# A hybrid attention kernel: order of the head, four constant products, and three instead of four products for each group of experts

## The chip, the cores and the metric

The kernel runs on one core of a Trainium2 chip. The metric is device microseconds (us) of one execution. A core has five engines that work side by side and wait for each other through semaphores: TensorE (PE, the matrix products), VectorE (DVE), ScalarE (ACT), GpSimd (POOL) and SyncE (SP, which only issues DMAs here). PE's products go to PSUM; the other engines bring them from there to SBUF.

## What is computed

```python
x = x + wo @ (softmax(k.T q) v)          # q, k, v = wq x, wk x, wv x: 32 channels; 4 images, 64 channels, 1024 pixels
t = tokens(x)                            # 4 x 1024 tokens of 64
u = layernorm(t);  t = t + softmax(u u.T) u
w = layernorm(t);  p = softmax(w @ router_w + router_b)        # 8 experts
top_p, top_i = top_k(p, 2);  top_p = top_p / sum(top_p)
t = t + sum over the two of top_p * (w @ expert_w[top_i] + expert_b[top_i])
```

All is fp32 in and out. A product that must be near fp32 is made of several products of rounded parts: a number is split into a high part (rounded) and a low part (the rest).

## The kernel before

The four images b = 0 to 3 go through the same stages, staggered: while PE makes the first attention of one image it makes the maxima, the second attention or the experts of others. The order on every engine is written out by hand, one call after another. Each engine works off its calls in that order.

**The ring.** Most of PE's results go into a ring of three PSUM buffers of two banks each. `ORDER` lists every use of the ring in PE's order; use n has buffer n mod 3, and `take` lets PE wait until the reader of use n - 3 is done. So the order in `HEAD`, `FIRST` and so on must be that of PE's calls, and it fixes for each use whose release it waits for.

**The head (image 0, and the start of image 1).** `project_qk` makes q or k of an image: two halves of 512 columns, two products each. `project_v(b, a)` makes one half of v together with the transposed input: eight products of 96 columns into `acc1` or `acc2`. `max_scores` makes a tile of scores whose row maxima DVE takes (`row_max`). When all eight tiles of an image are done, DVE negates the maxima (`negate_max`, semaphore `s_nm`), PE turns them into a row (`max_row` on PE, eight products of 128 columns), and ACT and DVE copy one half of that row each (`max_row` on ACT and DVE, `s_mrow`). Then `scores1(b, j)` can start, ACT takes exponentials (`exp1`), and `weigh_pair1` multiplies two tiles of them by v.

A projected q or k is rounded by ACT (`round_q`, `round_k`, `s_qr`, `s_kr`), then DVE writes the low part (`split_q`, `split_k`, `s_qs`, `s_ks`); only then can `max_scores` of that image start. ACT's `values(b, a)` brings a half of v out of PSUM (two copies, `s_vx`). DVE's order in the head stays: `row_max` of image 0, `negate_max(0)`, `split_q(1)`, `max_row(0)`, `split_k(1)`, two small copies of wo (behind PE's `transpose` into `acc2`), then `row_max(1, ...)`.

`keep_clock(n)` issues n products of constants (512 columns, f16) into `acc1` that nobody reads. It is called at the very start; `acc1` and `acc2` are free behind `wait_ge(s_vx, 4 * B)`.

**The experts.** `experts(b, g)` makes 128 x 1024 numbers: for two token tiles (h = 0, 1) the products with all 8 experts. Its operands are `w_hi`, `w_lo` (tokens) and `e1`, `e2` (expert weights); the half h has 64 rows of its own and a bank of its own. There are 16 such groups, four in each image. DVE's `weigh_experts(b, g)` multiplies a group by the gates (`s_prod`); POOL adds the experts up (`sum_pair`, then `residual`, which gives `y`) for images 0 and 1, and `y_transposed(b)` brings y back on PE. For images 2 and 3 PE adds the experts up itself (`add_experts`), with POOL or DVE halving them first. The gates come from `route(b)` on PE and `top2(b)`, some twenty small instructions on DVE. `w_transposed(b)` waits for the second norm: `att2_transposed` on PE, `tokens2`, `stats_of_2` on DVE, a power on POOL (`rstd`), `normalize2` on DVE.

Of the kernel before, what the change touches and what calls it, by code (L numbers as in the profile page):

```python
# [24 lines left out]
P = 128  # L25
# [13 lines left out]
def per_tile(name, b):  # L39
    return [(f"{name}{t}", b) for t in range(T)]  # L40

HEAD = [("w3", 0), ("q", 0), ("k", 0)] + per_tile("mx", 0) + [("q", 1), ("k", 1), ("mr", 0)]

FIRST = [("st0", 0), ("st1", 0), ("mx0", 1), ("st2", 0), ("mx1", 1), ("st3", 0), ("mx2", 1), ("mx3", 1), ("st4", 0),
         ("mx4", 1), ("st5", 0), ("mx5", 1), ("st6", 0), ("mx6", 1), ("st7", 0), ("mx7", 1), ("mr", 1), ("po", 0)]
# [22 lines left out]
TAIL = [("e1", 2), ("e2", 2), ("wT", 3), ("e3", 2), ("rt", 3), ("e0", 3), ("e1", 3), ("e2", 3), ("e3", 3)]  # L70
ORDER = HEAD + FIRST + SECOND + THIRD + FOURTH + FIFTH + SIXTH + SEVENTH + EIGHTH + TAIL
PLACE = {use: (n % RING, n) for n, use in enumerate(ORDER)}
# [6 lines left out]
def col(tile):  # L79
    return (tile % 2) * CHUNK + (tile // 2) * P  # L80


def build(nc, x, wq, wk, wv, wo, rw, rb, ew, eb, out):
    ctx = ExitStack()
    with ctx:
        def sb(name, shape, dt=F32):
            return ctx.enter_context(nc.sbuf_tensor(name, shape, dt))
# [4 lines left out]
        def two(name, shape, dt=F32):  # L92
            return [sb(f"{name}_{n}", shape, dt) for n in range(2)]
# [9 lines left out]
        w3 = sb("w3", [ROW, 2, C])  # L103
# [7 lines left out]
        e1 = sb("e1", [P, E * C], F32R)  # L111
        e2 = sb("e2", [P, E * C], F32R)
# [22 lines left out]
        w_hi = two("w_hi", [P, CHUNK], F32R)  # L135
        w_lo = two("w_lo", [P, CHUNK], F32R)
# [137 lines left out]
        def filled(engine, name, b):  # L274
            buf, n = PLACE[(name, b)]
            engine.wait_ge(s_fill, n + 1)
            return ring[:, buf]

        def flat(buf):
            return buf.rearrange("p a n -> p (a n)")  # L280
# [147 lines left out]
        def _(pe):  # L428
            taken = iter(range(len(ORDER)))

            def take(name, b):
                buf, n = PLACE[(name, b)]
                assert n == next(taken), (name, b)
                if n >= RING:
                    pe.wait_ge(*release(*ORDER[n - RING]))
                return ring[:, buf]

            def project_qk(name, b):
                which = "qk".index(name)
                buf = take(name, b)  # L440
                if b:
                    pe.wait_ge(s_xs, b + 2)
                for h in range(2):
                    if b == 0 and which == 0:
                        pe.wait_ge(s_xs, h + 1)
                    rows = xst[b][:, h * CHUNK:(h + 1) * CHUNK]
                    pe.matmul(buf[0:ROW, h, :], w1[:, which].rearrange("p r m -> p (r m)"), rows, start=True, stop=False)  # L447
                    mm = pe.matmul(buf[0:ROW, h, :], w2[:, which].rearrange("p r m -> p (r m)"), rows, start=False, stop=True)
                    if b == 0 and h == 0:
                        mm.then_inc(s_qk0, 1)  # L450
                mm.then_inc(s_fill, 1)

            def project_v(b, a):

                bank = v_at[a]
                if b:
                    pe.wait_ge(s_xs, b + 2)
                    pe.wait_ge(s_vx, 4 * (b - 1) + 2 * a + 2)
                for t in range(T // 2):
                    tile = a * (T // 2) + t  # L460
                    toks = xst[b][:, col(tile):col(tile) + P]
                    o = t * (M + C)
                    pe.matmul(bank[:, o:o + M + C], toks, vx1[:, :], start=True, stop=False)
                    mm = pe.matmul(bank[:, o:o + M + C], toks, vx2[:, :], start=False, stop=True)
                mm.then_inc(s_vp, 1)

            def max_scores(b, tile):
                buf = take(f"mx{tile}", b)
                if tile == 0:
                    pe.wait_ge(s_qs, b + 2)  # L470
                    pe.wait_ge(s_ks, b + 2)
                home = b % 2
                for h in range(2):
                    mm = pe.matmul(buf[:, h, :], kst[home][0:ROW, col(tile):col(tile) + P],  # L474
                                   qst[home][0:ROW, h * CHUNK:(h + 1) * CHUNK], start=True, stop=True)
                mm.then_inc(s_fill, 1)

            def max_row(b):
                buf = take("mr", b)
                pe.wait_ge(s_nm, 2 * (b + 1))  # L480
                for tile in range(T):
                    c = col(tile)
                    mm = pe.matmul(flat(buf)[0:ROW + 2, c:c + P], nmax[:, tile, :], ident_r[:, :], start=True, stop=True)  # L483
                mm.then_inc(s_fill, 1)

            def scores1(b, j):
                buf = take(f"st{j}", b)
                if j == 0:
                    pe.wait_ge(s_mrow, 2 * (b + 1))
                home = b % 2  # L490
                for h in range(2):
                    mm = pe.matmul(buf[:, h, :], qst[home][0:ROW + 2, col(j):col(j) + P],  # L492
                                   kst[home][0:ROW + 2, h * CHUNK:(h + 1) * CHUNK], start=True, stop=True)
                mm.then_inc(s_fill, 1)
# [108 lines left out]
            def experts(b, g):  # L603

                buf = take(f"e{g}", b)
                products = [(w, e) for w in (w_hi[b % 2], w_lo[b % 2]) for e in (e1, e2)]
                for n, (w, e) in enumerate(products):
                    for h in range(2):
                        rows = slice(h * C, (h + 1) * C)
                        mm = pe.matmul(buf[:, h, :], w[rows, g * P:(g + 1) * P], e[rows, :], start=(n == 0), stop=(n == 3))  # L610
                mm.then_inc(s_fill, 1)

            def gates_transposed(b):
# [36 lines left out]
            buf = take("w3", 0)  # L650
# [18 lines left out]
            project_v(2, 1)  # L669
            max_scores(0, 7)  # L670
            project_qk("q", 1)
            project_qk("k", 1)
            project_v(3, 0)
            max_row(0)
            project_v(3, 1)


            scores1(0, 0)
            scores1(0, 1)
            pe.wait_ge(s_wol, 2 * 16)  # L680
            pe.wait_ge(s_vx, 4 * B)
            pe.transpose(acc2[:, 0:C], wo4[:, :, :].rearrange("p a m -> p (a m)"), ident[0:C, 0:C]).then_inc(s_woT, 1)
            max_scores(1, 0)
            scores1(0, 2)
            weigh_pair1(0, 0)
# [95 lines left out]
            scores2(1, 4)  # L781
            weigh_pair2(1, 2)
            experts(0, 0)
            scores2(1, 5)
            u_transposed(2)
            max_scores(3, 7)
            experts(0, 1)
            scores2(1, 6)
            weigh_pair2(1, 4)
            experts(0, 2)  # L790
            scores2(1, 7)
            max_row(3)
# [101 lines left out]
        def _(act):  # L894
# [4 lines left out]
            def round_q(b):  # L899
                act.activation(qst[b % 2][0:ROW, :], flat(filled(act, "q", b))[0:ROW, :], ACT.Copy).then_inc(s_qr, 1)  # L900

            def round_k(b):
                act.activation(kst[b % 2][0:ROW, :], flat(filled(act, "k", b))[0:ROW, :], ACT.Copy).then_inc(s_kr, 1)

            def values(b, a):
                act.wait_ge(s_vp, 2 * b + a + 1)
                tiles = slice(a * (T // 2), (a + 1) * (T // 2))
                b4 = v_at[a][:, 0:(T // 2) * (M + C)].rearrange("p (t c) -> p t c", c=M + C)
                act.activation(val[b][:, tiles, 0:M], b4[:, :, 0:M], ACT.Copy).then_inc(s_vx, 1)
                act.activation(xt[b][:, tiles, :], b4[:, :, M:M + C], ACT.Copy).then_inc(s_vx, 1)  # L910

            def max_row(b):
                buf = filled(act, "mr", b)
                act.activation(kst[b % 2][ROW:ROW + 2, 0:CHUNK], buf[ROW:ROW + 2, 0, :], ACT.Copy).then_inc(s_mrow, 1)
# [56 lines left out]
            buf = filled(act, "w3", 0)  # L971
# [4 lines left out]
            for name, dst, s_rounded in (("q", qst[0], s_qr), ("k", kst[0], s_kr)):  # L976
                k, used = PLACE[(name, 0)]
# [14 lines left out]
            values(2, 0)  # L992
            values(2, 1)
            round_q(1)
            round_k(1)
            values(3, 0)
            max_row(0)
            values(3, 1)

            for j in range(4):  # L1000
                exp1(0, j)
# [3 lines left out]
            for h in range(2):  # L1005
                rows = slice(h * C, (h + 1) * C)
# [104 lines left out]
            b = B - 1  # L1111
# [336 lines left out]
```

## Time and profile before

| | us |
|---|---|
| median of 3 runs (208.2, 208.34, 466.2) | 208.34 |
| the profiled execution: its own time | 209.9 |
| its span, first to last instruction | 207.8 |
| PE busy in it | 195.0 |
| DVE busy | 142.5 |
| ACT busy | 108.3 |
| POOL busy | 62.9 |

The profile is one execution recorded by the hardware. Its span leaves out what lies before the first and behind the last instruction. A matmul's end in it is modelled and products overlap, so a row's duration is longer than the step from one product to the next; "busy" counts overlapping instructions once. The mean granted TensorE clock over the span is 0.992 of full speed.

### The profile page before, as it was taken

How to read it: one execution, taken by the hardware profiler on the slowest of the kernel's cores; microseconds unless marked ns; L12 is line 12 of the kernel's file. 1: busy time of each engine (PE TensorE's matmuls, PEld its weight loads, DVE VectorE, ACT ScalarE, POOL GpSimd, SP SyncE). 2: the span in 40 equal slices, each digit the busy share in tenths (PEclk: the TensorE clock that was granted, in tenths of full speed). 3: DMA queues.
4: the chain of work that ended last, by engine and by line, in shares of the span. 5: the costliest groups of instructions: out<-in, count | busy, mean ns of one | idle time of the engine just before them, and what ended most of it. 6: DMA issues, size and time to landing. Idle time of an engine off the chain costs nothing.

```text
span 207.8 us, 3044 instructions
## 1 busy us (share of the span) xinstructions
PE 195.0 (94%) x1121; PEld 100.0 (48%) x1121; DVE 142.5 (69%) x359; ACT 108.3 (52%) x172; POOL 62.9 (30%) x79
## 2 busy tenths in 40 slices
PE   7899999999999899998989999899999999899993
PEld 2678634354434334433433554353444334377882
DVE  3889736778846994793688855628794361998980
ACT  3765825548945466564367456566563875301010
POOL 8394000003000300021003479700369760026160
PEclk9999979999999999999999999999999999999999
DMA  4890000000000000000000000110000002000021
GB/s 112 204 156 0 3 0 0 2 2 3 0 0 0 0 3 0 0 0 3 0 2 0 3 2 0 24 26 0 3 0 3 0 0 52 0 3 0 0 54 51
DMA packets 3502, 3.69 MB, mean 18 GB/s; under 512 B 2208, under 2 KB 2464, under 8 KB 3488
## 3 DMA queue, kind: packets, MB, share of 16 engines
q1 hardware_dynamic: 3248, 3.45, 7.5%
q8 instruction: 9, 0.15, 0.3%
q10 hardware_dynamic: 240, 0.05, 0.1%
q14 instruction: 5, 0.04, 0.1%
HBM read 2.45 MB, written 1.05 MB: 17 GB/s over the span
## 4 chain that ended last, share of the span: by engine, by line
PE 66%; DVE 22%; POOL 4%; issue 3%; ACT 2%; DMA 1%; SPq 0%; DVEq 0%; POOLq 0%
PE acc L499 20%; PE ring L563 9%; PE ring L610 6%; PE ring L474 6%; DVE rowmax L1136 6%; PE ring L492 5%; POOL sm L372 4%; PE acc L640 3%; PE ring L536 2%; DVE stats L1169 2%; PE ring L547 2%; PE ring L599 2%; PE ring L483 2%; DVE tok L1215 2%; PE ring L447 1%
## 5 line engine op out<-in xcount | busy, mean ns | idle before, releaser
L372 POOL TENSOR_TENSOR sm<-sm,minus_half 128x8 f32<-128x8 f32 x8 | 15.8, 1975 | 117.2 <-DVE sm L1179 117.2
L920 ACT ACTIVATE prob<-ring,shift 128x1024 f32<-128x1024 f32 x32 | 35.6, 1112 | 25.0 <-PE ring L563 24.7
L1136 DVE TENSOR_REDUCE rowmax<-ring 128x1 f32<-128x1024 f32 x32 | 38.0, 1218 | 13.9 <-PE ring L474 13.8
L917 ACT ACTIVATE prob<-ring 128x1024 f32<-128x1024 f32 x32 | 32.1, 1023 | 21.3 <-PE ring L492 21.0
L499 PE MATMUL acc<-prob,val 128*64 128x512 f32 x128 | 31.8, 619 | 0.0
L499 PE MATMUL acc<-prob,u 128*64 128x512 f32 x128 | 31.2, 606 | 0.2 <-ACT prob L920 0.2
L1275 DVE TENSOR_TENSOR prod<-ring,gate 128x1024 f32<-128x1024 f32 x16 | 19.3, 1219 | 6.7 <-PE ring L610 6.7
L474 PE MATMUL ring<-qst,kst 96*128 96x512 f32 x64 | 22.3, 436 | 1.0 <-DVE rowmax L1136 0.8
L492 PE MATMUL ring<-kst,qst 98*128 98x512 f32 x64 | 21.8, 431 | 0.9 <-DVE kst L1133 0.5
L563 PE MATMUL ring<-zsw,zst 64*128 64x512 f16 x64 | 19.4, 376 | 0.0
L563 PE MATMUL ring<-zst,zsw 64*128 64x512 f16 x64 | 19.2, 376 | 0.0
L492 PEld LDWEIGHTS ring<-kst,qst 98*128 98x128 f32 x64 | 10.7, 193 | 11.8 <-ACT prob L917 5.9
L499 PEld LDWEIGHTS acc<-prob,val 128*64 128x64 f32 x128 | 7.9, 139 | 16.1 <-issue 13.3
L499 PEld LDWEIGHTS acc<-prob,u 128*64 128x64 f32 x128 | 7.7, 136 | 15.6 <-issue 12.9
L474 PEld LDWEIGHTS ring<-qst,kst 96*128 96x128 f32 x64 | 10.2, 190 | 9.1 <-issue 4.0
L384 POOL TENSOR_TENSOR half<-prod 128x512 f32<-128x512 f32 x8 | 10.6, 1322 | 8.4 <-DVE prod L1275 8.2
L563 PE MATMUL ring<-zst 64*128 64x512 f16 x32 | 12.3, 386 | 0.7 <-DVE rowmax L1136 0.4
L610 PE MATMUL ring<-e,w_hi 64*128 64x512 f32 x64 | 12.4, 443 | 0.0
L563 PE MATMUL ring<-zsw 64*128 64x512 f16 x32 | 12.4, 386 | 0.0
L610 PE MATMUL ring<-e,w_lo 64*128 64x512 f32 x64 | 10.9, 394 | 0.0
L563 PEld LDWEIGHTS ring<-zst 64*128 64x128 f16 x32 | 3.0, 92 | 13.3 <-issue 6.5
L423 POOL TENSOR_TENSOR prod<-prod 128x512 f32<-128x512 f32 x6 | 7.6, 1278 | 5.8 <-DVE prod L1275 4.8
(160 smaller groups left out, 323.3 us busy)
## 6 DMA issues: line engine op xcount, KB each, us to landing
xin<-in_x SPq DMA_DIRECT2D x6, 256.0 KB, 4.9
out<-ob SPq DMA_DIRECT2D x6, 128.0 KB, 2.5
xin<-in_x SPq DMA_DIRECT2D x4, 128.0 KB, 2.8
e_in<-in_L_ffn_expert_w SPq DMA_DIRECT2D x2, 128.0 KB
out<-ob SPq DMA_DIRECT2D x4, 64.0 KB, 2.0
eb_in<-in_L_ffn_expert_b SPq DMA_DIRECT2D x8, 2.0 KB
wo<-in_L_conv_wo SPq DMA_DIRECT2D x2, 8.0 KB, 2.2
r_in<-in_L_ffn_router_w SPq DMA_DIRECT2D x2, 2.0 KB
```

The lines of the kernel that those rows point to most:

```text
L372: pool.tensor_tensor(sm[:, 3, :], sm[:, 2, :], minus_half[:, :], ALU.pow).then_inc(s_rs, 1)
L384: pool.tensor_tensor(half[:, :, :, :], p[:, 0:E // 2], p[:, E // 2:E], ALU.add).then_inc(s_half, 1)
L423: pool.tensor_tensor(prod[:, g, 0:E // 2], prod[:, g, 0:E // 2], prod[:, g, E // 2:E], ALU.add).then_inc(s_half, 1)
L474: mm = pe.matmul(buf[:, h, :], kst[home][0:ROW, col(tile):col(tile) + P], qst[home][0:ROW, h * CHUNK:(h + 1) * CHUNK], start=True, stop=True)
L492: mm = pe.matmul(buf[:, h, :], qst[home][0:ROW + 2, col(j):col(j) + P], kst[home][0:ROW + 2, h * CHUNK:(h + 1) * CHUNK], start=True, stop= ...
L499: mm = pe.matmul(acc[h * C:(h + 1) * C, :], stationary[:, j, :], prob[:, j % DEEP, h * CHUNK:(h + 1) * CHUNK], start=(j == 0), stop=(j == ...
L563: mm = pe.matmul(buf[:, h, :], held[h][rows, col(j):col(j) + P], moving[h][rows, h * CHUNK:(h + 1) * CHUNK], start=(n == 0), stop=(n == 2))
L610: mm = pe.matmul(buf[:, h, :], w[rows, g * P:(g + 1) * P], e[rows, :], start=(n == 0), stop=(n == 3))
L917: act.activation(prob1[:, j % DEEP, :], flat(filled(act, f"st{j}", b)), ACT.Exp).then_inc(s_p1, 1)
L920: act.activation(prob2[:, j % DEEP, :], flat(filled(act, f"s{j}", b)), ACT.Exp, bias=shift[:, :], accum_out=rsum2[b % 2][:, j:j + 1]).then ...
L1136: dve.tensor_reduce(rowmax[:, tile:tile + 1], flat(filled(dve, f"mx{tile}", b)), AX.X, ALU.max).then_inc(s_mx, 1)
L1275: dve.tensor_tensor(prod[:, g].rearrange("p e h c -> p h e c"), buf.rearrange("p h (e c) -> p h e c", c=C), gates, ALU.mult).then_inc(s_pr ...
```

## The change

Three edits. In the head, PE makes k of image 1 behind `max_row(0)`, and both halves of v of image 3 ahead of it; `HEAD` and ACT's list follow. Behind the transpose of wo four constant products are issued. `experts` leaves out the product of the two low parts, so a group has three products for each half in place of four.

```diff
-HEAD = [("w3", 0), ("q", 0), ("k", 0)] + per_tile("mx", 0) + [("q", 1), ("k", 1), ("mr", 0)]
+HEAD = [("w3", 0), ("q", 0), ("k", 0)] + per_tile("mx", 0) + [("q", 1), ("mr", 0), ("k", 1)]
...
             def experts(b, g):
                 buf = take(f"e{g}", b)
-                products = [(w, e) for w in (w_hi[b % 2], w_lo[b % 2]) for e in (e1, e2)]
+                products = [(w_hi[b % 2], e1), (w_hi[b % 2], e2), (w_lo[b % 2], e1)]
                 for n, (w, e) in enumerate(products):
                     for h in range(2):
                         rows = slice(h * C, (h + 1) * C)
-                        mm = pe.matmul(buf[:, h, :], w[rows, g * P:(g + 1) * P], e[rows, :], start=(n == 0), stop=(n == 3))
+                        mm = pe.matmul(buf[:, h, :], w[rows, g * P:(g + 1) * P], e[rows, :], start=(n == 0), stop=(n == 2))
                 mm.then_inc(s_fill, 1)
...
             project_qk("q", 1)
+            project_v(3, 0)
+            project_v(3, 1)
+            max_row(0)
             project_qk("k", 1)
-            project_v(3, 0)
-            max_row(0)
-            project_v(3, 1)
             scores1(0, 0)
             scores1(0, 1)
             pe.wait_ge(s_wol, 2 * 16)
             pe.wait_ge(s_vx, 4 * B)
             pe.transpose(acc2[:, 0:C], wo4[:, :, :].rearrange("p a m -> p (a m)"), ident[0:C, 0:C]).then_inc(s_woT, 1)
+            keep_clock(4)
             max_scores(1, 0)
...
             round_q(1)
+            values(3, 0)
+            values(3, 1)
+            max_row(0)
             round_k(1)
-            values(3, 0)
-            max_row(0)
-            values(3, 1)
```

## Rows read from the trace of the kernel before

**Rows 1.** The page's parts 1 and 4: PE's busy time; the last chain by engine.
```profile
PE 195.0 (94%) x1121; PEld 100.0 (48%) x1121; DVE 142.5 (69%) x359; ACT 108.3 (52%) x172; POOL 62.9 (30%) x79
...
PE 66%; DVE 22%; POOL 4%; issue 3%; ACT 2%; DMA 1%; SPq 0%; DVEq 0%; POOLq 0%
```

**Rows 2.** Windows of the head: stretch, length, busy us per engine, PEclk, DMA share, GB/s.
```profile
24.50:25.00 0.50, 0.50 (x3) 0.14 (x2) 0.00 (x0) 0.36 (x1) 0.00 (x0) 1.00 0.00 0
...
25.50:28.50 3.00, 3.00 (x8) 1.19 (x8) 1.56 (x4) 1.58 (x2) 0.00 (x0) 0.50 0.00 0
...
20.00:23.00 3.00, 3.00 (x27) 2.79 (x25) 2.57 (x6) 2.77 (x5) 0.00 (x0) 1.00 0.03 5
```

**Rows 3.** Timeline of PE, head: start us, us, engine, line, out<-in [idle before <-releaser].
```profile
21.35 0.87 PE L483 MATMUL ring<-ident_r,nmax 128*98 128x128 f32 x8
22.06 0.26 PE L463 MATMUL acc<-vx,xst 128*128 128x96 f32 x1
...
23.10 0.70 PE L492 MATMUL ring<-kst,qst 98*128 98x512 f32 x2
24.26 0.73 PE L492 MATMUL ring<-kst,qst 98*128 98x512 f32 x2 [0.46 <-DVE kst L1133]
...
25.13 1.07 PE L474 MATMUL ring<-qst,kst 96*128 96x512 f32 x2
...
29.70 0.74 PE L474 MATMUL ring<-qst,kst 96*128 96x512 f32 x2
```

**Rows 4.** Timeline of ACT and of DVE in the same stretch.
```profile
20.72 1.02 ACT L903 ACTIVATE kst<-ring 96x1024 fp32r<-96x1024 f32 x1
...
22.26 0.70 DVE L1149 CAST kst<-ring 2x512 fp32r<-2x512 f32 x1 [0.19 <-PE ring L483]
22.99 1.22 DVE L1133 TENSOR_TENSOR kst<-ring,kst 32x1024 fp32r<-32x1024 f32 x1
```

**Rows 5.** The chain that ended last: start us, us, what.
```profile
20.45 0.23 PE ring L448
...
32.51 0.47 PE ring L492 x2
32.98 1.87 PE acc L499 x8
```

**Rows 6.** Timeline of PE at the start: three constant products.
```profile
4.97 0.81 PE L646 MATMUL acc<-filler 128*128 128x512 f16 x3
```

**Rows 7.** Timeline of PE: the halves of two groups of experts of image 2.
```profile
182.59 0.63 PE L610 MATMUL ring<-e,w_lo 64*128 64x512 f32 x4
...
183.06 0.63 PE L610 MATMUL ring<-e,w_hi 64*128 64x512 f32 x4
```

**Rows 8.** Timeline of POOL, DVE and PE where image 0's sums meet image 1's norm.
```profile
123.42 1.30 POOL L384 TENSOR_TENSOR half<-prod 128x512 f32<-128x512 f32 x1 [0.39 <-DVE prod L1275]
...
128.86 1.28 POOL L392 TENSOR_TENSOR yres<-ysum,tok 128x512 f32<-128x512 f32 x1
128.91 1.79 DVE L1215 TENSOR_TENSOR tok<-odiv,tok 128x512 f32<-128x512 f32 x1
...
130.22 1.61 POOL L397 TENSOR_TENSOR y<-yres,ybias 128x512 f32<-128x512 f32 x1
...
131.97 0.63 PE L572 MATMUL ring<-ident,y 128*128 128x128 f32 x4 [0.91 <-POOL y L397]
```

**Rows 9.** Timeline of DVE and PE: image 1's experts beside image 3's first norm.
```profile
153.47 1.10 DVE L1197 TENSOR_TENSOR uhl<-u,uhl 128x512 f16<-128x512 f32 x1
...
154.72 1.05 PE L547 MATMUL ring<-ident_h,uhl 128*128 128x128 f16 x16 [0.25 <-DVE uhl L1197]
```

**Rows 10.** Timeline of the tail: DVE's weighing, PE's last group of experts.
```profile
190.47 1.22 DVE L1275 TENSOR_TENSOR prod<-ring,gate 128x1024 f32<-128x1024 f32 x1
...
195.91 4.62 DVE L1275 TENSOR_TENSOR prod<-ring,gate 128x1024 f32<-128x1024 f32 x4
...
197.22 0.73 PE L610 MATMUL ring<-e,w_hi 64*128 64x512 f32 x4
```

## The prediction, made before the changed kernel was run

> **What bounds the kernel now.** First the page: PE is busy for 195.0 of 207.8 us, and the chain that ended last lies on PE for 66% and on DVE for 22% of the span [rows 1]. So PE's time is worth most, but not everywhere; each edit is priced in its own stretch. Then the windows of the head, for the clock. From 20 to 25 PE's clock stands at 1.00, that is 2.4 GHz; from 25.5 to 28.5 it stands at 0.50, that is 1.2 GHz, while PE is busy without a break [rows 2]. Ahead of the fall PE did 24 short products (a half of v, the row of maxima, the other half of v), two pairs of scores, and waited 0.46 us for DVE's `split_k(1)` [rows 3]. Then the timelines of ACT and DVE for what the first products of image 1 wait for [rows 4], the chain for prices at full clock [rows 5], and the stretches with experts, to see in each whether PE, DVE or POOL comes last [rows 7 to 10].
>
> **The head: the late k.** On PE, k (four products) changes places with the second half of v (eight short ones). k's chain step is 0.23 us [rows 5], so four are 0.92; a half of v takes from 22.06 to shortly before the scores at 23.10, also some 0.9 [rows 3]. So `max_row(0)` starts where it did, at 21.35, and k starts in v's old place, 22.06, and is done at about 23.15. On ACT `values(3, 0)` and `values(3, 1)` now fall into the 1.02 us that `round_k` held from 20.72 [rows 4] and behind it; the second ends at about 22.2, when the row of maxima is only just there, so ACT's `max_row` is not later, and DVE's half of it ends at 22.96 as before [rows 4]. `scores1(0, 0)` waits for that and keeps its 23.10; k now covers this wait on PE. In the ring the row of maxima takes the buffer of tile 6 and k that of tile 7; both were read before DVE negated the maxima. `scores1(0, 1)` now waits for the row's release, not k's, so the 0.46 us ahead of 24.26 are gone [rows 3].
>
> What is late next: `round_k(1)` starts at 23.2 in place of 20.72 and ends at 24.2, `split_k(1)` follows to 25.45 in place of 24.21 [rows 4], so `max_scores(1, 0)` starts at 25.5, against 25.13 [rows 3]: 0.4 us late. Behind `split_k` on DVE stand the copies of wo and `row_max(1, 0)`; the copies are four tiny instructions, done at about 26.1, when that tile is made. Behind `round_k` on ACT stands `exp1(0, 0)`, 0.25 us late, which `weigh_pair1(0, 0)` does not need before 26.4. No DMA moves.
>
> **The head: the constants.** Three took 0.81 us [rows 6], so four are at most 1.1. They start behind the transpose of wo, at 24.3, and end at 25.2 to 25.4: inside the wait for `split_k`. They cost nothing while that wait is there; if it were gone they would cost their 0.9 to 1.1.
>
> **The head: the clock.** In the new order the stretch ahead of 25.5 has k, two scores and the constants, all of 512 columns, without gaps. I take it that the clock stays. Then a tile of maxima, a tile of scores and two tiles of weighing cost 0.47 + 0.47 + 1.87 = 2.81 us [rows 5] where they cost 29.70 - 25.13 = 4.57 [rows 3], and the next tile starts at 25.52 + 2.81 = 28.33 in place of 29.70: **1.37 us won**. The bounds: 1.76 if `max_scores(1, 0)` were not late; a loss of 0.39 if the clock falls all the same. I take the value near the upper end, since k alone fills the place in which PE waited. From there on every engine follows PE, and all inputs are long in, so the gain reaches the end.
>
> The Trainium skill (TensorE: Matmul & The Clock Gate, "Why this matters for your kernels") puts the fall down to long pauses between bursts of products. This trace does not agree: the longest pause ahead of the fall is 0.46 us [rows 3]. By the page the new order would have nothing to win in the clock, which is the rival "the clock falls all the same".
>
> **Three products for each group.** The halves h = 0 and 1 overlap: a half group of four products steps 183.06 - 182.59 = 0.47 us [rows 7], 0.2325 a pair. Two products less are one pair: 0.2325 us in each of 16 groups, 3.7 in all if PE came last everywhere. Nothing else changes in a group, the semaphore sits on the last product as before. The floor is nothing, where another engine comes last. By image:
>
> Image 0 (114 to 125): PE comes last around all four, 0.93 at first sight. But POOL's sums feed `y_transposed(0)`, for which PE already waits 0.91 us at 131.97 [rows 8], and POOL gains less. Its second sum comes behind a `row_max` on DVE and gains only the first group's 0.23; its third had idled 0.39 [rows 8], of which 0.07 is the usual gap, so it gains 0.23 + 0.32 = 0.55, and from there POOL is busy without a break up to y. I take **0.55**; ends 0.4 and 0.93. The lower end has a cause: DVE's tok took 1.79 us, and 1.23 of them passed until POOL's yres was done, which had begun 0.05 us ahead of it [rows 8]. DVE will now come 0.93 earlier and POOL 0.55, so DVE comes first, and POOL's y can lose some 0.2. The Trainium skill (SBUF — State Buffer, "Who interferes with whom") says that DVE and POOL share a pair of ports under a lock and whoever comes first keeps it; the row agrees.
>
> Image 1 (148 to 160.5): the first group hands over to DVE, which gains its 0.23. The second lies ahead of `u_transposed(3)`, for which PE waits 0.25 us on DVE's low part, ending at 154.57 [rows 9]; what PE wins there it waits longer, 0. The third and fourth lie on PE: **0.70** in all.
>
> Images 2 and 3 (from 177): `top2(2)`, the norm and `top2(3)` on DVE set the pace. The last group of image 2 lies ahead of `route(3)`, but DVE is in `weigh_experts(2, 3)` until 191.7 anyway [rows 10]. The first three of image 3 lie ahead of its last, which must wait for DVE's first weighing, 195.91 + 1.23 = 197.14, and starts at 197.22 [rows 10]: nothing won so far. Only that last group shortens the end: **0.25** with the little around it; ends 0 and 0.5.
>
> **Sum.** 1.37 + 0.55 + 0.70 + 0.25 = 2.87 us off a span of 207.8. The profiled execution took 209.9, the median is 208.34, 0.54 above the span; I take the gain off the median: 205.5.
>
> **The rivals.**
> Every group counts in full (POOL and DVE follow, no lock): 16 x 0.2325 = 3.72, with the head 5.09, gives 203.2. For it speaks PE's 66% of the chain; against it the waits of PE on POOL and on DVE's low part [rows 8, 9] and the tail's DVE [rows 10].
> The clock falls all the same: the head loses 0.39 in place of winning 1.37, the experts give 1.50, so 208.34 - 1.11 = 207.2. For it: v and the row of maxima now stand in one block, 24 short products from about 19.6; against it: dense work behind them.
> Slower than before: that block makes the clock fall already at the row of maxima, and it stays low past the constants. Then k takes twice its 0.92, the two scores twice 0.94 and the constants some 1.8, which with the transpose fills PE from 22.06 to about 27.8; `max_scores(1, 0)` started at 25.13 and is 2.7 late, and the weighing is as slow as before: 2.7 - 1.5 = 1.2 lost, 209.5. It decides from the point at which the head loses more than the experts' 1.50. Against it: the clock was 1.00 all through 20 to 23 with 27 products, most of them short [rows 2].
> The lock goes against POOL or DVE in other places too, some tenths of a us each: 206.1 at most.
>
> **How the numbers follow.** My forecast has a chance of 0.66, with a range of its own from 204.6 to 206.2; full exposure 0.10, the clock that falls all the same 0.11, slower 0.04, the locks 0.09. The range from 204.2 to 207.3 leaves out full exposure and the slower case, and holds some 0.84. A change of 2% is 4.2 us, about what a measurement of this kernel can tell from none: faster by more than that only with full exposure, 0.10; slower by more, 0.02, as no case above reaches 212.5; within it 0.88.
>
> **What would show it.** Clock 1.00 from 25 to 29, and the second tile of maxima of image 1 at about 28.3; `max_scores(1, 0)` at 25.5, `split_k(1)` ending just ahead of it. A group of experts on PE shorter by 0.23. PE's wait at `y_transposed(0)` longer than 0.91, at `u_transposed(3)` longer than 0.25; `top2(2)` starting 2.6 earlier, and no gain between it and the last group. Wrong would be: a clock of 0.50 anywhere else, above all at 131, where PE waits longest, which costs up to the 1.76 that it cost in the head; or k's late split holding PE beyond 25.5.

## The result, and the profile after

The changed kernel takes 206.86 us (median of 4 executions, 206.78 to 206.94), the kernel before 208.27 beside it; the ratio is 0.9934, 95% interval 0.9914 to 0.9953. That is 1.4 us faster, within 2%, and about half of the 2.8 that the prediction gave. The profiled execution moved by twice as much: its span is 204.8 us against 207.8, 3.0 less.

Of the 84 executions of the kernel before that were timed beside the other kernels, 51 took 208.13 to 208.73 us (their median, 208.27, is called the usual time below), 22 took 209.66 to 210.34 and 11 more than 211, and the profiled execution, at 209.9, is one like the 22.

The page after, parts 1, 2 and 4: busy time of the engines, the granted clock in tenths by slice, the chain by engine.

```profile
PE 190.6 (93%) x1093; PEld 96.8 (47%) x1093; DVE 142.6 (70%) x359; ACT 108.1 (53%) x172; POOL 62.9 (31%) x79
...
PEclk9999999999999999999999999999999999999999
...
PE 63%; DVE 23%; POOL 6%; issue 3%; ACT 2%; DMA 1%; SPq 0%; DVEq 0%; POOLq 0%
```

PE lost 4.4 us of busy time [rows 1], part of it work (32 products less, 4 constants more), part of it the stretch at half clock. The granted clock stands at nine tenths or more in every slice; its mean is 1.000. The windows of the head (stretch, length, busy us by engine, then the clock):

```profile
20.00:23.00 3.00, 3.00 (x26) 2.56 (x25) 2.65 (x5) 2.42 (x6) 0.00 (x0) 1.00 0.00 0
...
25.50:28.50 3.00, 2.88 (x12) 1.16 (x12) 1.79 (x5) 1.57 (x2) 0.00 (x0) 1.00 0.00 0
```

Where [rows 2] had 0.50 stands 1.00. The timeline of PE in the head, after:

```profile
21.34 0.87 PE L483 MATMUL ring<-ident_r,nmax 128*98 128x128 f32 x8
22.05 0.42 PE L447 MATMUL ring<-xst,w 128*96 128x512 f32 x1
...
23.09 1.15 PE L492 MATMUL ring<-kst,qst 98*128 98x512 f32 x4
24.17 0.27 PE L681 MATMUL acc<-ident,wo 64*128 64x64 f32 x1
24.38 1.04 PE L646 MATMUL acc<-filler 128*128 128x512 f16 x4
25.62 0.70 PE L474 MATMUL ring<-qst,kst 96*128 96x512 f32 x2 [0.21 <-DVE kst L1133]
...
26.71 1.94 PE L499 MATMUL acc<-prob,val 128*64 128x512 f32 x8
28.58 0.73 PE L474 MATMUL ring<-qst,kst 96*128 96x512 f32 x2
```

and of ACT and DVE:

```profile
23.20 1.02 ACT L903 ACTIVATE kst<-ring 96x1024 fp32r<-96x1024 f32 x1 [0.36 <-PE ring L448]
...
22.25 0.70 DVE L1149 CAST kst<-ring 2x512 fp32r<-2x512 f32 x1
24.25 1.22 DVE L1133 TENSOR_TENSOR kst<-ring,kst 32x1024 fp32r<-32x1024 f32 x1 [1.31 <-PE ring L492]
```

The head went as it was worked out, nearly to the tenth: row of maxima at 21.34 (21.35), k at 22.05 (22.06), both tiles of scores at 23.09 without a pause, `round_k` at 23.20 (23.2), `split_k` done at 25.47 (25.45), `max_scores(1, 0)` at 25.62 (25.5). The second tile of maxima, at 28.58, came later than the 28.33 that was worked out; against the profiled execution of before that is 29.70 - 28.58 = 1.12 us earlier. The question is why the clock's part of that is missing from the median.

### The profile page after: what moved, and what is told of

Same layout as the page of the kernel before. It is cut to its first block, busy times and chain, and to the rows that moved or that the text cites. A ratio compares the mean times of both kernels' runs of the same rounds, so it can differ in the third digit from the quotient of the medians.

```text
span 204.8 us, 2988 instructions
## 1 busy us (share of the span) xinstructions
PE 190.6 (93%) x1093; PEld 96.8 (47%) x1093; DVE 142.6 (70%) x359; ACT 108.1 (53%) x172; POOL 62.9 (31%) x79
## 4 chain that ended last, share of the span: by engine, by line
PE 63%; DVE 23%; POOL 6%; issue 3%; ACT 2%; DMA 1%; SPq 0%; DVEq 0%; POOLq 0%
PE acc L499 20%; PE ring L563 9%; PE ring L474 6%; DVE rowmax L1136 6%; PE ring L492 6%; PE ring L610 3%; POOL sm L372 3%; PE acc L640 2%; PE ring L536 2%; DVE prod L1275 2%; PE ring L547 2%; PE ring L483 2%; DVE stats L1169 2%; PE ring L447 2%; DMA xin<-in_x 1%
## 5 line engine op out<-in xcount | busy, mean ns | idle before, releaser
L499 PE MATMUL acc<-prob,val 128*64 128x512 f32 x128 | 31.0, 605 | 0.0
L492 PE MATMUL ring<-kst,qst 98*128 98x512 f32 x64 | 21.1, 422 | 0.4 <-DVE rowmax L1136 0.4
L1169 DVE BATCH_NORM_STATS2 stats<-tok 128x6 f32<-128x64 f32 x64 | 8.9, 211 | 0.2
```

Source lines behind the costliest of these rows:

```text
L499: mm = pe.matmul(acc[h * C:(h + 1) * C, :], stationary[:, j, :], prob[:, j % DEEP, h * CHUNK:(h + 1) * CHUNK], start=(j == 0), stop=(j == ...
L1169: last = dve.bn_stats(stats[:, tile, :], tok[:, tile, :])
```

## The experiments

**Theory A**: the fall of the granted clock to 0.50 at 25 us ("the fall" from here on) belongs to some executions of the kernel before, the profiled one among them. The usual one runs there at full clock, so the head had nothing to win in it and only the lateness of k shows. **Theory B**: the fall is in every execution, the head won its 1.1 to 1.4 us, and the changed kernel loses as much somewhere else. Four kernels ran side by side.

**The kernel before, unchanged, once more.**

> The kernel before, unchanged, timed and profiled again. Theory A (the fall of the clock at 25 us belonged to the one profiled execution of before): its usual executions run at 1.00 there, their spans are about 206.2 us (the median 208.27 less the 2.07 us that lie around the span in the changed kernel, 206.87 - 204.8), the first tile of maxima of image 1 to the second takes about 2.8 us; an execution with a mean clock of 0.992 takes about 209.9. Theory B (the fall is in every execution, and the changed kernel loses 1.5 us outside the span): mean clock 0.992, span 207.8 and 208.3 us together.

Its 12 executions (beyond the 84): 9 from 208.17 to 208.73, one at 209.77, two above 211. This time the profiled execution is one of the nine (208.59, span 206.5). The timeline of PE in its head:

```profile
25.48 0.73 PE L474 MATMUL ring<-qst,kst 96*128 96x512 f32 x2
26.05 0.63 PE L492 MATMUL ring<-kst,qst 98*128 98x512 f32 x2
26.61 1.94 PE L499 MATMUL acc<-prob,val 128*64 128x512 f32 x8
28.48 0.72 PE L474 MATMUL ring<-qst,kst 96*128 96x512 f32 x2
```

From the first to the second tile of maxima it is 3.00 us here, where [rows 3] have 29.70 - 25.13 = 4.57: the same instructions, 1.57 us less. Theory A.

**The head alone.**

```diff
 (the changed kernel, with)
-                products = [(w_hi[b % 2], e1), (w_hi[b % 2], e2), (w_lo[b % 2], e1)]
+                products = [(w, e) for w in (w_hi[b % 2], w_lo[b % 2]) for e in (e1, e2)]
```

> The new order of the head and the four constants, with four products for each group of experts as before. Theory A: no clock to win in the usual execution, and max_scores(1, 0) comes about 0.45 us later (25.62 against 25.13), so 208.27 + 0.45 = 208.7, slightly slower than before. Theory B: the head wins its 1.1 to 1.4 us: about 207.0.

208.69 us (12 executions, 208.56 to 208.99; ratio to before 0.9995, interval 0.997 to 1.002). Against the usual 208.27 that is 0.42 us more, what theory A gave for a k that is 0.45 late; theory B's 207.0 is out. What the head did give shows in the spread: none of the 12 lies in a second group above the others.

**The experts alone.**

```diff
 (the kernel before, with)
-                products = [(w, e) for w in (w_hi[b % 2], w_lo[b % 2]) for e in (e1, e2)]
+                products = [(w_hi[b % 2], e1), (w_hi[b % 2], e2), (w_lo[b % 2], e1)]
...
-... stop=(n == 3))
+... stop=(n == 2))
```

> Three products for each group of experts, the head as before. Theory A: the profiles of before and after, compared behind the head, show 2.93 - 1.12 = 1.81 us won by the experts, so 208.27 - 1.8 = 206.45, faster than the whole change (206.86). Theory B: the head made the gain, the experts' is given back: 208.2.

206.51 us (ratio 0.9889, interval 0.9852 to 0.9926; five of its six executions from 206.38 to 206.60, the sixth at 210.43). This third of the change alone beats the whole one by 0.35 us.

**The constants alone**, behind the transpose of wo, in the order of before.

```diff
 pe.transpose(acc2[:, 0:C], wo4[...], ident[0:C, 0:C]).then_inc(s_woT, 1)
+keep_clock(4)
```

> Only the four constant products behind the transpose of wo, all else as before. In this order nothing waits there, k is split at 24.21, so they stand on PE's path: four steps of about 0.22 us. Theory A: 208.27 + 0.9 = 209.1. Theory B: the clock is kept, max_scores(1, 0) starts at 26.05 and the weighing ends 2.81 us later, at 28.9 in place of 29.70: 207.5.

209.14 us, and nine of the twelve from 208.96 to 209.32, with a median of 209.12: the constants cost 0.85 us, about their four steps, where no wait covers them. The other three took 210.51 to 211.03, 1.4 to 1.9 more, each at a mean granted clock of 0.992, that of the first profiled execution of before. So in this place the constants don't prevent a fall; none of the three was profiled, so where it came isn't shown. In [rows 2] it comes between 25.0 and 25.5; here the constants start at 25.10.

**Which groups count.** The terms of the experts were then tried one at a time.

```diff
-products = [(w, e) for w in (...) for e in (e1, e2)]
+products = [(w, e) for w in (...) for e in (e1, e2)][:3 if b == 0 else 4]      # b >= 2 in the second kernel
...
-stop=(n == 3)
+stop=(n == len(products) - 1)
```

> Three products only in the four groups of image 0, all else as before. The prediction's step (POOL's sums hold y_transposed(0)) gives 0.55 us: 207.75. The profiles of before and after show 0.85 between the first weighing and the second attention of image 2: 207.45. All four groups in full would be 0.93: 207.35.

207.64 us, nine of eleven executions from 207.34 to 207.74 with a median of 207.59: 0.68 less than the usual 208.27. The timeline of PE and of POOL where the prediction saw the limit:

```profile
25.36 0.72 PE L474 MATMUL ring<-qst,kst 96*128 96x512 f32 x2
...
130.07 0.63 PE L572 MATMUL ring<-ident,y 128*128 128x128 f32 x4 [1.27 <-POOL y L397]
...
126.97 1.60 POOL L392 TENSOR_TENSOR yres<-ysum,tok 128x512 f32<-128x512 f32 x1
128.65 1.27 POOL L397 TENSOR_TENSOR y<-yres,ybias 128x512 f32<-128x512 f32 x1
```

In the second profile of before `y_transposed(0)` starts at 130.73 with the same 0.91 of waiting as in [rows 8]. So it comes 0.66 us earlier here, some 0.55 when the different starts of the two executions are allowed for (0.12, by the first tile of maxima at 25.48 and 25.36), and the wait has grown to 1.27.

> Three products only in the eight groups of images 2 and 3. If DVE sets the pace there and only the last group counts: 0.25 us less, 208.0. If PE set it: eight pairs, 1.86 us less, 206.4.

Six of eleven executions took 207.92 to 208.75, with a median of 208.08 (208.01 without the one at 208.75, whose mean clock was 0.992): 0.2 to 0.3 less than before, not 1.86. PE does not set the pace in the tail. The other five took 209.56 to 210.15, the profiled one among them (209.63), and its profile caught the fall (clock 0.50 from 25.5 to 28.5):

```profile
core 0: 207.6 us, clock 0.989
...
25.19 1.07 PE L474 MATMUL ring<-qst,kst 96*128 96x512 f32 x2
...
27.04 2.79 PE L499 MATMUL acc<-prob,val 128*64 128x512 f32 x8
29.76 0.74 PE L474 MATMUL ring<-qst,kst 96*128 96x512 f32 x2
```

These are the 1.07 and 4.57 us of [rows 3] in another kernel with the same head, in an execution that took 1.55 us more than the median of the six.

**The order without the constants**, with four products.

```diff
 (the head alone, with)
-            keep_clock(4)
```

> The new order of the head without the four constants, four products for each group. If the constants only fill the wait for split_k(1), the usual execution is that of the head alone, 208.7. If dense k and scores are enough to keep the clock, no execution lies some 1.6 us above the others; if the constants keep it, about a third do, as with before (10 of its 29 executions took 209.7 to 211).

208.75 us; ten of eleven executions from 208.55 to 208.99 and one at 218.7, whose mean clock was 0.945 and which was not profiled. PE now waits where the constants stood:

```profile
24.39 0.27 PE L681 MATMUL acc<-ident,wo 64*128 64x64 f32 x1
25.75 0.70 PE L474 MATMUL ring<-qst,kst 96*128 96x512 f32 x2 [1.09 <-DVE kst L1132]
```

So the constants of the change cost nothing and gave nothing that these executions show: in ten of eleven the order alone keeps the clock, with PE idle for 1.09 us.

**Half of v in the wait**: k early as before, the row of maxima right behind it, the second half of v between the two tiles of scores, three products.

```diff
 (the experts alone, with)
             project_qk("k", 1)
-            project_v(3, 0)
             max_row(0)
-            project_v(3, 1)
+            project_v(3, 0)
             scores1(0, 0)
+            project_v(3, 1)
             scores1(0, 1)
+            max_scores(1, 0)
+            scores1(0, 2)
             ... (the transpose of wo with its waits)
-            max_scores(1, 0)
-            scores1(0, 2)
```

ACT's list follows: `max_row(0)`, `values(3, 0)`, `exp1(0, 0)`, `values(3, 1)`.

> Three products for each group; in the head k stays early, the row of maxima comes right behind it, and the second half of v of image 3 stands between the two tiles of scores, where PE waited 0.46 us for split_k(1); the transpose of wo moves behind the third tile of scores; no constants. If the wait is what the head can still give, the second tile of maxima comes 0.4 us earlier than in the experts' change alone (206.5): 206.1. If ACT or DVE comes last there, nothing: 206.5.

206.65 us, four of five executions from 206.33 to 206.69: nothing won over the experts alone. Its profiled execution was the fifth (210.28), with the clock down in several places, from between 23.5 and 24 on. Ahead of that it shows two new waits:

```profile
21.07 0.88 PE L483 MATMUL ring<-ident_r,nmax 128*98 128x128 f32 x8 [0.52 <-DVE nmax L1142]
...
23.05 0.69 PE L492 MATMUL ring<-kst,qst 98*128 98x512 f32 x2 [0.22 <-DVE kst L1147]
```

Without a half of v ahead of it the row of maxima waits for DVE's `negate_max`, and the scores for DVE's half of the row; the first tile of scores starts at 23.05, hardly earlier than 23.10 [rows 3]. So the move opened as much waiting ahead of the scores as it meant to fill behind them. What came last behind 23.5 in the other four stays open.

**Two constants in the wait**, with three products: the place where PE idles for 0.46 us [rows 3].

```diff
 (the experts alone, with)
             scores1(0, 0)
+            pe.wait_ge(s_vx, 14)
+            keep_clock(2)
             scores1(0, 1)
```

> Three products for each group, the head in the order of before, and two constant products between scores1(0, 0) and scores1(0, 1), where PE waits 0.46 us for split_k(1). If they fit into the wait and keep the clock: 206.5 as with the experts' change alone, and no execution some 1.6 us above. If they don't keep it: 206.5, and about a third of the executions near 208.1. If they hold up scores1(0, 1): 206.6 to 206.8.

206.55 us (five executions, 206.34 to 206.83; ratio 0.9914, interval 0.9900 to 0.9928). Timeline of PE:

```profile
23.63 0.60 PE L646 MATMUL acc<-filler 128*128 128x512 f16 x2
24.25 0.73 PE L492 MATMUL ring<-kst,qst 98*128 98x512 f32 x2
...
25.12 0.73 PE L474 MATMUL ring<-qst,kst 96*128 96x512 f32 x2
```

They fit: `max_scores(1, 0)` at 25.12, as early as in [rows 3]. Beside it the experts alone and the changed kernel ran again:

> The experts' change alone, once more, for how its executions are spread: usual ones at 206.5, and, since the head is that of before, about a third near 208.1, where the clock falls at 25 us.

> The changed kernel once more on the same chip: 206.9, and no execution near 208.5, since the clock does not fall in its head. The mean over many executions may then be no worse than that of the experts' change alone (two thirds at 206.5, a third at 208.1: 207.0).

The experts alone: 206.66, six of nine executions from 206.38 to 206.98, two at 208.2 and one at 209.71. The changed kernel: 206.85, all five from 206.77 to 207.04. And the two constants once more:

> The two constants in the wait, with three products for each group, once more, for the spread: five executions without a fall come about by chance in one case of eight if a third of the executions fall. If the constants keep the clock: again 206.3 to 206.9 and none near 208.1. If they don't: about a third near 208.1.

206.39 us (ratio 0.989, interval 0.9844 to 0.9936), five from 206.21 to 206.47 and one at 207.65. So this version beats both the kernel before and the changed one, the latter by 0.3 to 0.5 us; against the experts alone (206.51 and 206.66) it shows no clear gain. That it keeps the clock is not shown: one of its 11 executions lies 1.3 us above the others, at a mean clock of 0.992 like those with a fall, and one of 11 against 22 of 84 can be chance.

## Why the prediction was right or wrong

**The step that failed is the last one of the sum: "I take the gain off the median".** The 1.37 us of the head were worked out from an execution with the fall, and taken off a median of executions without it: against the median the head's term is 0.42 lost, not 1.37 won. The table of times before had the sign of it: the profiled execution took 209.9 and the median 208.34, 1.56 more, and that is what the fall costs. The prediction names both times, and that the median lies only 0.54 above the span, but does not ask why the profiled execution lies 2.1 above it. In the changed kernel time and span lie 2.07 apart (206.87 and 204.8), in the second profile of before 2.09 (208.59 and 206.5); so a median of 208.27 had a span of 206.2, not of 207.8, and the 1.6 missing were the half-clock stretch itself: 4.57 against 3.00 us.

**The head, price and size.** The path of k and its lateness were right. With the fall in the execution before, the head wins 1.12 in the profiles, 0.25 less than the 1.37: 0.10 because `max_scores(1, 0)` is 0.49 late rather than 0.39, and 0.15 because the stretch from it to the second tile of maxima takes 28.58 - 25.62 = 2.96 us and not 2.81, which were steps added up from another place of the chain. Without it, it loses 0.42 (the head alone), the prediction's own 0.39 for a clock that gives nothing. The rival "the clock falls all the same", 207.2, had the right loss for another reason: in the median the clock did not fall at all, before or after. That 206.86 lies inside the range is owed to the room that was left for this rival, not to the head's gain.

How often it falls in the head of before: 22 of 84 executions lie in the band 1.4 to 2.1 us above the usual (the fall itself is seen in the profiled ones alone). With the new order (the changed kernel twice, the head alone, the order without constants) none of 32 lies in such a band, one far above. So the new order takes a loss of some 1.6 us from one execution in four and costs 0.42 in all of them, and 22 of 84 times 1.6 is 0.42 too: in the mean the two cancel. Leaving out what lies more than 2.4 us above the lowest, the mean of before is 208.79, that of the changed kernel 206.87, and that of the experts alone (13 of 15 executions) 206.78. How the fall picks its executions was not tried.

**Three products for each group: 0.2325 a pair.** The timeline of PE after, groups of image 3:

```profile
189.28 0.63 PE L610 MATMUL ring<-e,w_hi 64*128 64x512 f32 x4
189.74 0.40 PE L610 MATMUL ring<-e,w_lo 64*128 64x512 f32 x2
189.97 0.63 PE L610 MATMUL ring<-e,w_hi 64*128 64x512 f32 x4
```

A group steps 0.69 us where it stepped 0.93 [rows 7]: right.

**Image 0, 0.55 with ends 0.4 and 0.93.** Right at `y_transposed(0)`, low by a third over the whole stretch. The rows of after that answer to [rows 8]:

```profile
126.85 0.79 DVE L1215 TENSOR_TENSOR tok<-odiv,tok 128x512 f32<-128x512 f32 x1
...
127.17 1.60 POOL L392 TENSOR_TENSOR yres<-ysum,tok 128x512 f32<-128x512 f32 x1
...
128.85 1.28 POOL L397 TENSOR_TENSOR y<-yres,ybias 128x512 f32<-128x512 f32 x1
...
130.27 0.63 PE L572 MATMUL ring<-ident,y 128*128 128x128 f32 x4 [1.27 <-POOL y L397]
```

`y_transposed(0)` came 131.97 - 130.27 = 1.70 us earlier, 0.58 beyond the head's 1.12: POOL holds PE, as worked out. DVE did come first this time, its tok took 0.79 in place of 1.79, and POOL's yres stretched to 1.60 while y shrank to 1.28: their sum, 2.88, is that of before (1.28 + 1.61) within 0.01, so the lock cost POOL nothing net. With the Trainium skill's rule (SBUF — State Buffer, "Who interferes with whom": who comes first keeps the ports) both orders agree. What was missed lies behind: PE's next wait is `w_transposed(1)`, and that one hangs on DVE's norm, not on POOL's y. Rows of before:

```profile
131.96 0.16 DVE L1173 SCALAR_TENSOR_TENSOR sm<-stats 128x8 f32<-128x8 f32 x1
...
134.91 0.69 DVE L1220 TENSOR_TENSOR wn<-cen,sm 128x512 f32<-128x512 f32 x1 [1.61 <-POOL sm L372]
...
135.75 0.63 PE L586 MATMUL ring<-ident,wn 128*128 128x128 f32 x4
```

and of after:

```profile
128.91 1.24 DVE L1173 SCALAR_TENSOR_TENSOR sm<-stats 128x8 f32<-128x8 f32 x1
...
132.93 0.69 DVE L1220 TENSOR_TENSOR wn<-cen,sm 128x512 f32<-128x512 f32 x1 [1.61 <-POOL sm L372]
...
133.77 0.63 PE L586 MATMUL ring<-ident,wn 128*128 128x128 f32 x4
```

In both `w_transposed(1)` starts 0.15 us behind the end of `wn`; the second profile of before marks it as a wait for `wn`. DVE's tok follows PE's `att2_transposed`, which stands ahead of `y_transposed(0)` and so had all four pairs: it came 128.91 - 126.85 = 2.06 us earlier, the head's 1.12 and 0.94. The wait for POOL did not go; it moved from tok (1.00 us less) to a small instruction of the norm beside POOL's y (L1173, 1.08 more), so the norm ends only 0.08 less early than it starts. `w_transposed(1)` comes 135.75 - 133.77 = 1.98 us earlier, and 0.86 are left of image 0. The kernel with three products in image 0 alone has the same rows: `w_transposed(1)` at 133.57 against 134.51 in the second profile of before, 0.94 earlier, some 0.8 with the starts allowed for. Its executions gave 0.68; what makes up the difference stays open.

**Image 1, 0.70 with nothing for the second group.** Right in the profiles: `route(2)` starts at 175.62 before and comes 2.68 us earlier after, so the distance grows by 0.70 from `w_transposed(1)` on, and PE's wait at `u_transposed(3)` grows from 0.25 [rows 9] to 0.49. A row of before, then two of after:

```profile
175.62 0.62 PE L599 MATMUL ring<-r_blk,w_hi 128*128 128x32 f32 x4
```

```profile
152.51 1.05 PE L547 MATMUL ring<-ident_h,uhl 128*128 128x128 f16 x16 [0.49 <-DVE uhl L1197]
...
172.94 0.62 PE L599 MATMUL ring<-r_blk,w_hi 128*128 128x32 f32 x4
```

Image 1 was not run alone.

**The tail, 0.25.** Right: from `route(2)` to the last copy on ACT the profiles' distance grows by 0.25, from 2.68 to 204.33 - 201.40 = 2.93, and the kernel with three products in images 2 and 3 alone gave 0.2 to 0.3. PE now waits for `top2(3)`, and the last group starts behind DVE's first weighing as before. A row of before, then rows of after:

```profile
204.33 0.38 ACT L1116 ACTIVATE ob<-acc 128x256 f32<-128x256 f32 x1 [2.18 <-PE acc L640]
```

```profile
193.23 4.62 DVE L1275 TENSOR_TENSOR prod<-ring,gate 128x1024 f32<-128x1024 f32 x4
...
193.29 0.30 PE L619 MATMUL acc<-ident,gate 128*128 128x128 f32 x1 [0.47 <-DVE gate L1264]
...
194.51 0.73 PE L610 MATMUL ring<-e,w_hi 64*128 64x512 f32 x4
...
201.40 0.38 ACT L1116 ACTIVATE ob<-acc 128x256 f32<-128x256 f32 x1 [2.18 <-PE acc L640]
```

One weighing takes 1.23 us, so the first ends at 193.23 + 1.23 = 194.46, and the group starts at 194.51; [rows 10] had 197.14 and 197.22.

**The sum put right.** The experts' three terms measure 0.86 + 0.70 + 0.25 = 1.81 between the profiles, and 208.27 - 206.5 = 1.8 in the executions (predicted 1.50). The experts alone against the second profile of before, both without the fall, give nearly the same split: 0.81, 0.68 and 0.25 with their starts allowed for (0.30). The head costs 0.42. 1.8 - 0.42 = 1.4, what the median moved.

**The rivals.** Full exposure (203.2) is out by the 0.2 of images 2 and 3. A clock that falls earlier and stays low (209.5) was not seen in the profiles of the new order. The locks elsewhere (206.1 at most) are not what is missing: the one that the rows show cost DVE's norm 0.08 us, and the experts gave more than their 1.50. The Trainium skill's rule (TensorE: Matmul & The Clock Gate, "Why this matters for your kernels": the fall comes of long pauses) does not describe this fall: PE was never idle for more than 0.46 us ahead of it [rows 3], while with 1.09 us of idleness in the order without constants ten of eleven executions show none.

## What to carry to other kernels

Compare the profiled execution's own time with the median before taking its rows for the usual case: if it is longer by as much as the stall that the change is to cure, the stall may be in that execution only, and its gain belongs to the mean, not the median. A product off the path is worth nothing however many there are: eight groups in a stretch where VectorE comes last gave 0.2 us, four in one where TensorE comes last around each of them 0.7. And the gain is settled at the last wait behind the work, not at the first: there another engine may come last. Work moved behind a wait as cover makes its own consumers late (0.42 us here), while two constants in the wait cost nothing; that they gave anything isn't shown.

## What the hardware showed that was not expected

The clock fell behind a stretch that the profile calls busy: 3.00 of 3.00 us from 20 to 23 [rows 2], mostly products of 96 and 128 columns, and then 0.46 us of waiting. Two profiled executions caught it there. By the times it came in about one execution of four of the same program: the 22 took 1.4 to 2.1 us more than the usual, at mean granted clocks of 0.988 to 0.992. With both halves of v and the row of maxima in one block, and k's and the scores' 512 columns close behind, 31 of 32 executions are without it. Why it comes in some executions and not in others stays open.

An instruction of 128 x 8 numbers on VectorE took 1.24 us in place of 0.16: it started 0.06 us behind GpSimd's y and ended about with it (128.91 + 1.24 against 128.85 + 1.28).
